# Two-layer gated cross-attention kernel: setup with the context transposes first, the minimum's chain divided, padded query features, and new orders on all engines

## The reference

```python
x = x + tanh(g_xattn[0]) * performer(layernorm(x), ctx, ctx, feats)       # 16 heads of 8, 32 random features
x = x + tanh(g_ffn[0])   * rwkv_ffn(layernorm(x), W_r, W_k, W_v, mu_r, mu_k)
x = x + tanh(g_xattn[1]) * class_attention(ctx, layernorm(x), w_kv, w_q, w_la, w_proj, b_proj, att_weight)
x = x + tanh(g_ffn[1])   * bitlinear_ffn(layernorm(x), w_gate, w_up, w_down)
# performer, causal linear attention:
q, k = q * scale, k * scale
h_k = -0.5 * sum(k * k);  k_stab = max(h_k)             # one maximum over everything
q' = exp(q @ feats) + eps;  k' = exp(h_k + k @ feats - k_stab) + eps
out[l] = q'[l] . sum_{j<=l} k'[j] v[j] / (q'[l] . sum_{j<=l} k'[j])
```

## Time and profile before

| what | before |
|---|---|
| median of 3 runs | 479.83 |
| lowest and highest run | 478.34 and 479.87 |
| the profiled execution, its own time | 478.8 |
| span of the profiled execution | 477.0 |
| busy PE, DVE, ACT, POOL | 435.7, 405.2, 353.5, 341.8 |
| mean granted clock of PE | 0.989 |

### The profile page before, as it was taken

How to read it: one execution, slowest core, us unless ns; L and a number is a source line. 1 busy time by engine, 2 the same in 40 slices (tenths; PEclk the granted TensorE clock), 3 DMA queues, 4 the chain that set the end, 5 groups by cost and what they waited for, 6 DMA issues and landing times.

```text
span 477.0 us, 18181 instructions
## 1 busy us (share of the span) xinstructions
PE 435.7 (91%) x7436; PEld 325.4 (68%) x7436; DVE 405.2 (85%) x1208; ACT 353.5 (74%) x765; POOL 341.8 (72%) x548
## 2 busy tenths in 40 slices
PE   3878989999989999998999999999999999888886
PEld 2256767677758686776867776777676867665675
DVE  6476758687999898999998989899998899998975
ACT  2243557758798887988789879897969695978763
POOL 7022556779689779689979796968787978886731
PEclk9979899999999999999999999999999999999999
DMA  6831201102111110130101010200100000000000
GB/s 180 208 82 40 54 20 36 47 18 59 31 25 30 35 43 21 34 101 19 32 23 43 21 28 14 65 21 20 47 19 2 21 2 19 8 12 12 4 12 24
DMA packets 33012, 18.26 MB, mean 38 GB/s; under 512 B 5280, under 2 KB 32800, under 8 KB 32928
## 3 DMA queue, kind: packets, MB, share of 16 engines
q1 hardware_dynamic: 32352, 17.07, 13.7%
q10 hardware_dynamic: 576, 0.02, 0.1%
HBM read 9.74 MB, written 2.10 MB: 25 GB/s over the span
## 4 chain that ended last, share of the span: by engine, by line
PE 39%; POOL 24%; DVE 17%; ACT 12%; issue 4%; DMA 2%; SPq 0%; POOLq 0%; ACTq 0%; DVEq 0%
PE MC L1575 6%; POOL call L439 6%; PE TP L1552 6%; PE FP L1484 5%; POOL call L419 5%; PE MA L1498 4%; PE SP L1543 2%; POOL ft L377 2%; DMA call<-in_ctx 2%; PE FP L1467 2%; PE FP L1471 2%; DVE WT L1028 2%; DVE mx L1071 2%; ACT ffn L720 2%; DVE emn L1090 2%
## 5 line engine op out<-in xcount | busy, mean ns | idle before, releaser
L1575 PEld LDWEIGHTS MC<-Vc,ET 128*64 128x64 f32 x2048 | 65.2, 138 | 17.6 <-issue 8.1
L1552 PE MATMUL TP<-ident,call 128*128 128x128 f32 x512 | 74.6, 278 | 2.8 <-POOL call L439 2.0
L1575 PE MATMUL MC<-Vc,ET 128*64 128x25 f32 x2048 | 71.5, 218 | 4.4 <-DVE n L1108 1.4
L1552 PEld LDWEIGHTS TP<-ident,call 128*128 128x128 f32 x512 | 56.7, 141 | 16.8 <-POOL call L439 5.8
L439 POOL TENSOR_TENSOR call<-call,Gs 128x1024 f32<-128x1024 f32 x32 | 60.9, 1904 | 1.5
L419 POOL TENSOR_TENSOR call<-call,rsh 128x1024 f32<-128x1024 f32 x32 | 60.9, 1905 | 1.4
L377 POOL TENSOR_SCALAR ft<-ft 128x512 f32<-128x512 f32 x64 | 39.9, 623 | 10.1 <-ACT ft L612 5.2
L1028 DVE TENSOR_TENSOR WT<-FP,mask 128x512 f32<-128x512 f32 x64 | 41.8, 681 | 5.9 <-PE FP L1484 5.8
L664 ACT ACTIVATE ET<-TP 128x512 f32<-128x512 f32 x64 | 36.5, 595 | 13.9 <-PE TP L1552 13.5
L1071 DVE TENSOR_REDUCE mx<-SP 128x16 f32<-128x1024 f32 x32 | 38.9, 1214 | 2.4 <-PE SP L1543 2.3
L1484 PEld LDWEIGHTS FP<-ft 32*64 32x64 f32 x2048 | 33.4, 135 | 10.9 <-DVE WT L1028 3.5
(11 more groups left out here) (218 smaller groups left out, 1093.8 us busy)
## 6 DMA issues: line engine op xcount, KB each, us to landing
Cd<-in_ctx SPq DMA_DIRECT2D x32, 128.0 KB, 2.7
call<-in_ctx SPq DMA_DIRECT2D x4, 512.0 KB, 8.2
xall<-in_x SPq DMA_DIRECT2D x4, 512.0 KB, 4.6
cz<-cT SPq DMA_DIRECT2D x64, 32.0 KB, 1.9
cz<-csq SPq DMA_DIRECT2D x64, 32.0 KB, 1.8
kX<-kT SPq DMA_DIRECT2D x128, 8.0 KB
out_x<-X SPq DMA_DIRECT2D x16, 128.0 KB, 1.9
ffn<-in_L_ffn_w_gate SPq DMA_DIRECT2D x1, 256.0 KB, 4.8
```

What stands on the lines that cost most here:

```text
L1552: last = pe.transpose(TP[:, c:c + P], src[:, c:c + P], ident[:, :])
L1575: last = mm(MC[64 * j:64 * j + 64, c + 32 * q:c + 32 * q + 25], weights[:, q, 64 * j:64 * j + 64], Vc[g.p][:, 2 * u + j, q, 0:25], start=T ...
```

## The change

1. **Setup.** The eight batches of context transposes are issued first, then the eight sums. The last steps of the minimum's chain become functions (`cmin_turn`, `cmin_spread` on PE, `cmin_last`, `bound` on DVE) that the lists call among the first groups' work. PE no longer waits for `nkst` before `values(G[0])`; ACT waits for it before its first exponential, and `gate_sums(0)` before it overwrites the bank.
2. **Padded query features.** `Rq2` holds, for each half of the rows and each `w`, the 32 rows of the random features with 32 rows of zeros beside them, so that the two query products take 64 rows as the key products do. Which 32 rows belong to which `(x, w)` is exchanged in `strips`, `ftp` and `features` accordingly.
3. **New orders** of all five lists, and waits added or dropped to fit (`add_X2`, `scaled`, `less`, `first`, `attend1`, `quant_kh`).

The functions of the diff in full, and of the five lists the first lines:

```diff
-        own = sb("own", [P, P])
-        Rq = sb("Rq", [P, P])
+        Rq2 = sb("Rq2", [P, 2, P])
...
+        Rq, own = X4[0][:, 0, :], X4[0][:, 1, :]
...
-                        r = 32 * (2 * w + x)
+                        r = 32 * (2 * x + w)
...
-            strips(G[0]); strips(G[1]); spread(G[0]); load(G[2]); spread(G[1]); strips(G[2]); strips(G[3])
-            load(G[3]); strips(G[4]); load(G[4]); load(G[5]); strips(G[5]); spread(G[2]); rows(2)
...
+            strips(G[0]); strips(G[1]); spread(G[0]); spread(G[1]); strips(G[2]); load(G[2]); load(G[3])
+            strips(G[3]); strips(G[4]); load(G[4]); strips(G[5]); load(G[5]); spread(G[2]); rows(2)
...
-                    f = ft[:, t, 2 * w:2 * w + 2, :]
+                    f = ft[:, t, w::2, :]
...
                 at(pool, s("vr"), g.k + 1)
+                at(pool, s("x2b"), g.k - 1)
...
                     at(pool, s("Gs"), g.k * 2 + 1)
-                    at(pool, s("zr"), g.k * 2 + 1)
...
-            rsA_chunk(1); ftp(G[0], 0); ftp(G[0], 1); add_X1(G[0]); rsB(G[0]); ftp(G[1], 0); ftp(G[1], 1)
-            masked(G[0]); add_X2(G[0]); rsC(G[0]); add_X1(G[1]); rsB(G[1]); ftp(G[2], 0); masked(G[1]); ftp(G[2], 1)
...
+            ftp(G[0], 0); ftp(G[0], 1); rsA_chunk(1); add_X1(G[0]); rsB(G[0]); ftp(G[1], 0); ftp(G[1], 1)
+            add_X2(G[0]); masked(G[0]); rsC(G[0]); add_X1(G[1]); masked(G[1]); rsB(G[1]); ftp(G[2], 0); ftp(G[2], 1)
...
+            shift(G[3], 1); rsB(G[5]); ffn_round(G[1], 0); shifted(G[3], 1); rsD(G[2]); scaled(G[3], 1); ftp(G[6], 0)
...
-                act.activation(ft[:, 0, 2 * w:2 * w + 2, :], f[:, 0], ACT.Exp).then_inc(s("fe"), 1)
-                act.activation(ft[:, 1, 2 * w:2 * w + 2, :], f[:, 1], ACT.Exp, bias=nkst[:, 0:1]).then_inc(s("fe"), 1)
+                act.activation(ft[:, 0, w::2, :], f[:, 0], ACT.Exp).then_inc(s("fe"), 1)
+                act.activation(ft[:, 1, w::2, :], f[:, 1], ACT.Exp, bias=nkst[:, 0:1]).then_inc(s("fe"), 1)
...
-            yA(G[0]); keys(G[0]); values1(G[0]); values0(G[0]); rows_T(G[0]); values1(G[1]); keys(G[1])
-            features(G[0], 0); yA(G[1]); features(G[0], 1); rows_T(G[1]); yA(G[2]); weights_T(0); features(G[1], 0)
...
+            keys(G[0]); values1(G[0]); yA(G[0]); values1(G[1]); rows_T(G[0]); keys(G[1])
+            act.wait_ge(s("nkst"), 1); features(G[0], 0); features(G[0], 1); yA(G[1]); values0(G[0]); rows_T(G[1])
+            yA(G[2]); values0(G[1]); features(G[1], 0); features(G[1], 1); yB(G[0]); rows_T(G[2]); shift_rows(G[0])
...
+            for r in range(4):
+                v.memset(Rq2[32 * r:32 * r + 32, 1 - r % 2, :], 0.0).then_inc(s("Rk"), 1)
...
+            for r in range(4):
+                v.tensor_copy(Rq2[32 * r:32 * r + 32, r % 2, :], Rq[32 * r:32 * r + 32, :]).then_inc(s("Rk"), 1)
...
-            chunk_A2(0)
             v.wait_ge(s("ss"), 8)
             v.tensor_reduce(cmin[:, 1:2], MC[:, :], op=ALU.min, axis=AX.X).then_inc(s("cmin"), 1)
             v.wait_ge(s("cmin"), 2)
             v.tensor_tensor(cmin2[:, :], cmin[:, 0:1], cmin[:, 1:2], ALU.min).then_inc(s("cmin"), 1)
...
+            chunk_A2(0)
+
+            def cmin_last():
+
+                v.wait_ge(s("cminP"), 1)
+                v.tensor_reduce(cmin1[:, :], MA[0:1, 0:P], op=ALU.min, axis=AX.X).then_inc(s("cmin"), 1)
+
+            def bound():
+
+                v.wait_ge(s("cminP"), 2)
+                v.tensor_scalar(nkst[:, :], MA[:, 0:1], 0.5 * S2, None, ALU.mult).then_inc(s("nkst"), 1)
...
                     at(v, s("mx"), g.k * 2 + 1)
+                    at(v, s("t2"), g.k * 4 - 2)
...
-                    at(v, s("oC"), g.k * 2 - 1)
                 elif u == 1:
                     at(v, s("r1"), g.k * 2 + 2)
+                    at(v, s("oC"), g.k * 2)
...
                 at(v, s("pr"), g.k + 1)
-                at(v, s("x2b"), g.k + 1)
...
+                at(v, s("hx0"), g.k * 5)
                 at(v, s("hx1"), g.k * 5)
+                at(v, s("am"), g.k * 3 + 2)
...
-            weights_sum(); chunk_A(1); weights_scale(); weights_round(0); gate_reduce(0); weights_rows()
-            weights_round(1); gate_reduce(1); gate_mean(); causal(G[0], 0); causal(G[0], 1); causal(G[0], 2)
...
+            cmin_last(); bound(); chunk_A(1); weights_sum(); weights_rows(); gate_reduce(0)
+            weights_scale(); weights_round(0); causal(G[0], 0); causal(G[0], 1); causal(G[0], 2); causal(G[0], 3)
...
-                if i == 3:
-                    pe.wait_ge(s("bones"), 1)
-                if i >= 4:
-                    sums(i - 4)
-            for i in range(4, 8):
+            pe.wait_ge(s("bones"), 1)
+            for i in range(8):
                 sums(i)
...
-                    r = 32 * (2 * w + x)
-                    mm(FP[:, 512 * x:512 * x + 256], Rq[r:r + 32, :], qT[r:r + 32, :], start=True, stop=True)
+                    mm(FP[:, 512 * x:512 * x + 256], Rq2[64 * x:64 * x + 64, w, :], qT[64 * x:64 * x + 64, :],
+                       start=True, stop=True)
...
-            pe.wait_ge(s("nkst"), 1)
             pe.wait_ge(s("zero"), 1)
-            values(G[0]); weights_rows(); rows_T(G[0]); zeros(4, TP, 1)
-            pe.wait_ge(s("Vc"), 4); values(G[1]); weights_total(); gate_sums(0)
-            pe.wait_ge(s("kTs"), 2); features(G[0], 0); zeros(18, TP, 1)
-            pe.wait_ge(s("fe"), 2); features(G[0], 1); zeros(5, TP, 1)
-            pe.wait_ge(s("setup"), 7); gate_sums(1); weights_turn(0); zeros(4, TP, 1); weights0(G[0], 0)
-            zeros(20, TP, 1)
+            pe.wait_ge(s("cst"), 4)
+            values(G[0]); cmin_turn(); weights_rows(); zeros(24, TP, 1)
+            pe.wait_ge(s("Vc"), 4); values(G[1]); rows_T(G[0]); cmin_spread(); zeros(19, TP, 1)
+            pe.wait_ge(s("kTs"), 2); features(G[0], 0); gate_sums(0)
+            pe.wait_ge(s("fe"), 2); features(G[0], 1); weights_total(); zeros(36, TP, 1); weights0(G[0], 0)
+            pe.wait_ge(s("setup"), 7); gate_sums(1); zeros(26, TP, 1)
             pe.wait_ge(s("WT"), 2); weights0(G[0], 1); out0(G[0], 0)
...
```

## The result

The changed kernel takes 474.24 (median of 4 runs, 473.52 to 475.42), the kernel before 479.85 on the same chip: the ratio is 0.9898, with a 95% interval of 0.9867 to 0.9929. So it is faster by 1.0%: 4.9 by the ratio, 5.6 by the two medians alone; the text goes by ratios. The forecast was 470.0, a gain of 9.9. The direction is right, the size is twice what came.

What follows compares the result with a forecast made beforehand. No single engine was taken as the bound: the chain hands over between engines, PE having least room. 478.8 - 6.5 (setup) - 4.5 (padding) + 0 (orders) + 1.5 (tail) = 469.3, put at 470.0; own range 465 to 474, outer 463 to 478.

Steps and rivals of the forecast that it cites:

- DVE takes PE's place: Rival in the loop: DVE becomes the bound, padding gives nothing and the tail gives back 2.5; 474.8, chance 0.22.
- the setup is no earlier: Rival in the setup: strips land later than before or loads fill the queues; 474.8, chance 0.04.
- Setup, -6.5: Setup term: first key products 6.6 earlier, 1.3 given back, 1.2 gained at the clock; -6.5, between -3.5 and -8.
- the chain from there to the first weights product stays the same: Setup step: from group 0's key products to its first weights product takes 6.2 as before, so that starts at 34.1.
- What is given back: Setup step: second gate sums and 26 zeros between the halves of group 0's weights products, where 20 zeros stood; +1.3.
- The 1.2 for the old half-clock stretch: Setup step: the second stretch at the lower clock, 54.8 to 58.3, should shrink; 1.2 gained of 0 to 1.75.
- do not change the sum there: Setup step: gate products and FFN-weight rounding, moved behind group 1's first products, still precede group 2's first weights product; costed nothing.
- Padding, -4.5: Query and key products of one shape save at most 7.7 of PE's time, 3.6 to 7.3 reaching the end; -4.5.
- New orders, 0: Loop term: reordering all five queues could close or grow PE's idle time, -9 to +9; taken as 0.
- I find no reason for one side: Loop: reordered steps mostly move one or two places, so neither gain nor loss was favoured within -9 to +9.
- Tail, +1.5: Tail term: reordered DVE steps and more zeros before the last products in the last group; +1.5, 0 to +3.
- The two steps on VectorE named for it: Tail: least(G15, 0) behind the other half's largest and less, 0 to 2.4 later; ffn_out(G14, 0) before ffn_h(G15, 0).

Runs made afterwards that it cites:

- old_setup: Changed kernel with sums of squares back between the transpose batches and PE waiting for the finished minimum before its first values product; 0.9975 of the kernel before.
- old_orders_mended: Kernel before with padding, new setup, VectorE's masks ahead of the second gate sums, gate's mean and second weight rounding, and group 0's strips issued early; 0.9963 of before, 476.38.
- orders_alone: Changed kernel with both the old setup and query products of 32 rows, leaving the new orders with their waits; 1.0076 of the kernel before.
- padded_in_old_order: Kernel before with only the padded query features, exchanged rows and wider query products added, setup and orders old; 0.9942 of the kernel before.
- narrow_queries: Changed kernel with its query products taken back to 32 rows; 1.0030 of the kernel before.
- after_again: Changed kernel unaltered, run again as the mark for a later comparison; 0.9913 of the kernel before.
- strips_early: Changed kernel with group 0's strips issued earlier on SP's queue, ahead of group 1's context rows and three weight loads; 0.9837 of the kernel before, 471.52.
- clock_held: Changed kernel with 52 zero products added in PE's wait for group 0's strips; 0.9874 of the kernel before.
- old_orders_gate_later: old_orders_mended with the gate's turn and spread and the second and third weight rounding moved behind group 1's weights products; 0.9881 of the kernel before, 473.24.

## Why the prediction was right and wrong, point by point

- **What bounds the kernel.** Right that PE has the least room and the chain hands over. The rivals "DVE takes PE's place" and "the setup is no earlier" both gave 474.8, almost the measured time, and both mechanisms are false: relieving VectorE changed nothing that could be measured, and the first weights product starts 4.0 earlier. VectorE has 28% of the chain and could give up 5 of its time all the same, so its steps there probably link POOL and PE; that is not shown.
- **Setup, -6.5: the mis-sized term; it measured -3.3.** The transposes, `values(G0)` (18.07 for 19.2) and `nkst` (23.37 for 24 to 26) came as worked out or a little earlier, and the strips did come last. (The minimum does not need the statistics of x, from which the text counted; they only stand ahead of it in VectorE's list.) The step that failed is that "the chain from there to the first weights product stays the same", at 6.2: it was 7.9, because the wait for the strips let the clock fall, 1.7. The text had foreseen the wait and still said that no row would stand at half clock after 20. The strips were 1.0 late as well (28.93 for 27.9): the place in SP's queue is the same, but one of their eight issues took 1.63 in place of 0.59. These two make -3.8 of -6.5. And of the 4.0 by which the first weights product comes earlier, 1.9 is there in old_setup too, whose trace is at the lower clock only from 26.0 to 29.3 where the kernel before is from 24.2 to 31.0. `weights0(G2, 0)` was to be six to seven earlier; it is 4.4.
- **What is given back.** 1.3 for `gate_sums(1)` and 26 zeros was about right: 3.64 between the two weights products of group 0, 2.57 before, 1.1 more. The 1.2 for the old half-clock stretch was right for the first trace of the changed kernel and wrong for the second, where one of 3.3 stands at 61.8: its coming and going is not understood, so that it went in the trace shown is luck.
- **Moved work at nothing.** That the gate's products and the rounding "do not change the sum there" was the wrong reading of the most useful part of the new orders: with this work left where it was, most of the start's gain is lost by group 1 (old_orders_mended, 7.4 to 1.1), to the waits for VectorE and to the clock after them.
- **Padding, -4.5.** It measured -2.8, -4.8 or -6.0, by what else is in the kernel, so the term holds, in part by luck: the granted clock is in these numbers and was not in the term. A joined call takes 1.07, not 1.02, 6.1 in all for 7.7. The share on the chain of the kernel before (47%) gave 3.6, near the 2.8 of the old orders. The loop from `weights0(G3, 0)` to `project(G12)` became 2.6 shorter (308.4 to 305.8), well inside the 9 that would have refuted the text.
- **New orders, 0, with the tail at +1.5: the other mis-sized term; they measured +3.6 alone.** The trace of orders_alone puts 2.4 of its longer time into the start of groups 1 to 3, about 1 into the loop and 1.7 into the tail (its profiled execution is 1.4 above its median). Part of this is again the clock: it is at 0.50 from 64.5 to 71.2, twice as long as the stretch of before at 54.8, and from 221.5 to 224.8 in the loop, where the trace of before has none. "I find no reason for one side" could not have seen this from the trace of before.
- **Tail, +1.5.** The size was right: from `project(G12)` to the end it is 76.0 before and 77.7 after. The two steps on VectorE named for it were tried and are not the cause; the third, more zeros ahead of the last products, was not tried, and it stays open.
- **The sum.** The terms were added as if each had its worth by itself. By themselves in the old kernel they are -2.8 (padding), +2.1 (setup on top of it) and +3.6 (orders), +2.9 in all; together they are -4.5. The padding pays alone; the setup costs 2.1 in the old orders and pays 3.3 in the new ones, and the orders cost 3.6 alone and pay 3.8 on top of padding and setup (0.9985 to 0.9905).
- **The rule against the padding.** The Trainium skill (TensorEngine Tiling (Array Packing), Performance Considerations) counts 32 rows as fourfold and 64 as twofold row tiling; read strictly, as the prediction's rival read it, the query pair would be slower at 64 rows. It is faster, 0.54 for 0.63. Another rule of the Trainium skill's page (TensorEngine Tiling (Array Packing), Tiling Modes) fits: changing the tiling mode drains the array. PEld's rows of the key products' loads in the loop, before and in padded_in_old_order (busy, mean ns, idle before):

```profile
L1471 PEld LDWEIGHTS FP<-cz,Rk 64*128 64x128 f32 x96 | 7.2, 184 | 8.0 <-issue 8.0
```

```profile
L1475 PEld LDWEIGHTS FP<-cz,Rk 64*128 64x128 f32 x96 | 9.3, 187 | 1.1
```

The wait of 8.0 in 24 calls ahead of these loads is 1.1 where both pairs have one shape. The changed kernel has the same 1.1; in narrow_queries the 8.0 is back.

## What to carry to other kernels

Before adding up the parts of a change, ask for each which other part must be there for it to pay: an earlier start is worth what the next waits on the in-order queues let through, and time taken from an engine is worth more or less by the orders it will run in. Its share of the chain is a hint there and no price: 28% gave VectorE's relief nothing that could be measured. A wait that a prediction itself foresees on TensorE should be priced with the clock behind it, and filled or removed. Before a difference of 1 or 2 between two traces is put down to an edit, compare where the granted clock fell in each. A rival that gives the right time is not thereby the right mechanism; a relief of the suspected engine tells.

## What was not expected of the hardware

After a wait of 3.49 the granted clock was 0.50 in the next 5.6, and with 52 zero products of 3.08 in that wait it stayed at 1.00, worth 1.7. In the loop PE waits 1.49 for VectorE ahead of one `ffn_dn`, up to 214.19 in the first trace of the changed kernel and up to 214.76 in the second; right behind it the clock was at 0.50 for 3.3 in the second (after_again, 215.4) and not in the first. Six of the other traces have such a stretch between 208 and 225. What decides it, no run tells. One of group 0's eight equal strip issues on SP's queue took 1.63 (changed kernel) or 1.54 (strips_early) and the others 0.59. In the kernel before and in the five other traces with the old setup all eight took 0.6; with the new setup ten of twelve traces have such a long issue (in clock_held two, of 0.80 and 0.95), and old_orders_mended and old_orders_gate_later have none. What holds it is not known.
